# Moving the spread of a small low-rank factor from ScalarE to VectorE, and asking for it once in the middle of a product

## The reference, cut to what matters

```
x1  = x + W[cond[b]].T @ x                 # 128 x 2048
Bx  = x1 @ B[id[b]].T                      # 128 x 16   (sum over the 2048 times)
out = x1 + Bx @ A[id[b]].T                 # 128 x 2048
```

## Time and profile before

| | us |
|---|---|
| median of three runs | 393.79 |
| the profiled execution, its own time | 395.34 |
| its span, first to last instruction | 393.5 |
| between the two | 1.84 |
| PE busy in it | 376.5 |
| DVE / ACT / POOL busy in it | 230.8 / 238.4 / 112.2 |
| mean granted clock of PE | 0.982 of full |

### The profile page before, as it was taken

The page is one execution under the profiler, slowest core; times in us unless marked ns, Lnnn a source line. Parts: engine busy times, 40 slices in busy tenths (PEclk is TensorE's granted clock), DMA queues, the critical chain, the costliest instruction groups (busy, mean ns, idle before and its releaser), DMA issues.

```text
span 393.5 us, 16869 instructions
## 1 busy us (share of the span) xinstructions
PE 376.5 (96%) x6170; PEld 354.3 (90%) x6170; DVE 230.8 (59%) x447; ACT 238.4 (61%) x579; POOL 112.2 (29%) x260
## 2 busy tenths in 40 slices
PE   7989989999999999999999999999999999999981
PEld 7979979999999999999999999999999999999871
DVE  0226762676555667755566775556677555667763
ACT  1566644666656666665666666566666666666541
POOL 2122330333332223333222333322233332223210
PEclk9999988999999999999999999999999999999996
DMA  7999997999999999999999999999999999999567
GB/s 272 417 362 347 407 409 277 345 415 386 406 414 412 408 416 415 415 404 414 404 418 410 416 405 410 414 405 409 414 415 414 410 406 406 415 403 413 223 250 277
DMA packets 28383, 152.24 MB, mean 387 GB/s; under 512 B 3153, under 2 KB 3154, under 8 KB 12242
## 3 DMA queue, kind: packets, MB, share of 16 engines
q1 hardware_dynamic: 28226, 151.79, 96.1%
q10 hardware_dynamic: 144, 0.26, 0.2%
HBM read 84.94 MB, written 67.11 MB: 386 GB/s over the span
## 4 chain that ended last, share of the span: by engine, by line
PE 93%; DMA 2%; issue 2%; ACT 1%; DVE 1%; POOL 1%; SPq 0%; POOLq 0%; DVEq 0%; ACTq 0%
PE bank L388 60%; PE bank L428 16%; PE bank L404 16%; DMA x_in<-in_x 2%; POOL z_pair L218 0%; ACT x_out L300 0%; DVE x_out L319 0%; ACT z_all L268 0%; POOL z_all L223 0%; ACT ft L256 0%; DVE z_pair L335 0%; DVE z_part L312 0%; DVE z_all L339 0%; SPq L134 0%; SPq L133 0%
## 5 line engine op out<-in xcount | busy, mean ns | idle before, releaser
L388 PE MATMUL bank<-m_sel,x_in 128*128 128x128 f32 x2048 | 240.8, 279 | 2.9 <-ACT ft L256 1.7
L388 PEld LDWEIGHTS bank<-m_sel,x_in 128*128 128x128 f32 x2048 | 234.1, 194 | 8.6 <-DVE x_out L319 2.7
L256 ACT COPY ft<-bank 128x512 f32<-128x512 f32 x256 | 146.1, 587 | 65.5 <-PE bank L388 63.5
L319 DVE TENSOR_TENSOR x_out<-bank,ft 128x512 f32<-128x512 f32 x253 | 154.3, 681 | 19.6 <-PE bank L428 19.5
L218 POOL TENSOR_TENSOR z_pair<-z_part 16x128 f32<-16x128 f32 x126 | 54.2, 446 | 217.0 <-DVE z_part L312 198.6
L312 DVE COPY z_part<-bank 16x128 f32<-16x128 f32 x126 | 36.2, 287 | 121.2 <-PE bank L404 119.2
L268 ACT COPY z_all<-z_all 16x128 f32<-16x128 f32 x189 | 56.0, 296 | 46.9 <-POOL z_all L223 43.8
L428 PE MATMUL bank<-z_all,at 16*128 16x128 f32 x2048 | 70.0, 282 | 2.8 <-issue 1.8
L428 PEld LDWEIGHTS bank<-z_all,at 16*128 16x128 f32 x2048 | 63.2, 187 | 10.1 <-issue 10.0
L404 PE MATMUL bank<-ft,ab_in 128*16 128x128 f32 x2048 | 65.6, 274 | 1.6 <-issue 1.6
L404 PEld LDWEIGHTS bank<-ft,ab_in 128*16 128x16 f32 x2048 | 51.4, 96 | 10.6 <-issue 5.1
(11 more groups left out here) (7 smaller groups left out, 0.9 us busy)
## 6 DMA issues: line engine op xcount, KB each, us to landing
x_in<-in_x SPq DMA_DIRECT2D x63, 1024.0 KB, 11.3
out<-x_out SPq DMA_DIRECT2D x62, 1024.0 KB, 10.1
ab_in<-in_lora SPq DMA_DIRECT2D x64, 256.0 KB, 10.0
out<-x_out SPq DMA_DIRECT2D x3, 512.0 KB, 4.3
w_all<-in_weights SPq DMA_DIRECT2D x1, 1024.0 KB, 4.9
x_in<-in_x SPq DMA_DIRECT2D x2, 512.0 KB, 6.9
out<-x_out SPq DMA_DIRECT2D x1, 256.0 KB, 4.6
out<-x_out ACTq DMA_DIRECT2D x1, 256.0 KB, 5.9
```

The lines of the kernel that those rows point to most:

```text
L256: nc.scalar.copy(ft[k][u][:], bank[f_bank_of(kind, i, u, final)][:]).then_inc(copied, 1)
L319: nc.vector.tensor_tensor(x_out[k][:, UNIT * u:UNIT * (u + 1)], bank[banks[u]][:], ft[k][u][:], ALU.add).then_inc(added, 1)
L388: last = nc.tensor.matmul(to[:, P * c:P * (c + 1)], x_in[k][:, UNIT * u + P * c:UNIT * u + P * (c + 1)], m_sel[k][:], start=(c == 0), stop ...
```

## The change: what it does

1. `place_z` leaves ACT in all normal rounds and goes to DVE, in the round after, behind the two turns of A (L328) and ahead of `take_z`: six copies of 16x128 a round. For batch 62, and for the split work of batch 63, ACT keeps it.
2. PE's waits are put elsewhere. What stood ahead of L404 (A and B loaded, banks free, z taken) and of L428 (A turned, z summed, z placed, banks free) goes. In its place PE waits ahead of the last unit (u = 3) of the second batch's product, the round's eighth unit, for: z of b-2 and b-1 placed, the copies of batch b, and the x of the next round's first batch with its W. Between z of b and z of b+1 there is still the wait for ACT's last copies, and between the two low-rank products one for z taken.
3. In the end part PE asks for z of batch 61 ahead of the fourth unit of batch 62, and the z sums of batches 62 and 63 ask unit by unit for their copies.
4. The second batch's `take_z` counts on a semaphore of its own (z_odd_taken).

```
 ACT:
     for i in range(ROUND):
         take_z(i, b + i, Z_BANKS[i])
-    for i in range(ROUND):
-        place_z(ROUND * kind + i, b + i)
 DVE:
     for i in range(ROUND):
         turn_a(ROUND * kind + i, b + i, q + 1)
+    if begun(b - ROUND):
+        for i in range(ROUND):
+            place_z(ROUND * (1 - kind) + i, b - ROUND + i)
     for i in range(ROUND):
         take_z(i, b + i, Z_BANKS[i])
+def place_z(k, b):
+    dve.wait_ge(z_summed, b + 1)
+    for u in range(1, UNITS):
+        nc.vector.tensor_copy(z_all[k][rows_of_unit(u), :], z_all[k][rows_of_unit(0), :]).then_inc(z_placed, 1)
 PE, normal_round:
-    for i in range(ROUND):
-        mix_units(kind, i, b + i, q + 1, False)
-    for i in range(ROUND):
-        sum_z(k + i, b + i, q + 1, Z_BANKS[i], UNITS * (b - BODY + 1) + i + 1, b + i - 1)
-    if begun(b - ROUND):
-        add_low_rank(other, b - ROUND, LOW_BANKS[kind][0], UNITS * (b - ROUND), 0)
-        add_low_rank(other + 1, b - ROUND + 1, LOW_BANKS[kind][1], 0, b + ROUND)
+    for u in range(UNITS):
+        mix_unit(kind, 0, u, b)
+    ask_for_x(k + 1, b + 1, q + 1)
+    for u in range(UNITS):
+        if u == UNITS - 1:
+            if begun(b - ROUND):
+                ask_for_z(b - ROUND + 1)
+            else:
+                pe.wait_ge(a_turned, b + ROUND)
+            pe.wait_ge(copied, UNITS * (b + 1))
+            ask_for_x(other, b + ROUND, q + 1 + kind)
+        mix_unit(kind, 1, u, b + 1)
+    for u in range(UNITS):
+        sum_unit(k, u, b, Z_BANKS[0])
+    pe.wait_ge(copied, UNITS * (b + ROUND))
+    for u in range(UNITS):
+        sum_unit(k + 1, u, b + 1, Z_BANKS[1])
+    if begun(b - ROUND):
+        add_low_rank(other, LOW_BANKS[kind][0])
+        pe.wait_ge(z_odd_taken, 2 * (b + ROUND))
+        add_low_rank(other + 1, LOW_BANKS[kind][1])
+def ask_for_z(b):
+    pe.wait_ge(z_placed, (UNITS - 1) * (b + 1))
 PE, the end:
+    for u in range(UNITS):
+        if u == UNITS - 1:
+            ask_for_z(b - 1)
+        mix_unit(1, 0, u, b, True)
+    for u in range(UNITS):
+        pe.wait_ge(copied, UNITS * b + u + 1)
+        sum_unit(ROUND, u, b, Z_BANKS[0])
+    add_low_rank(0, LAST_LOW)
```

More of the change, by code:

```diff
@@ L106, in cond_lora_residual @@
         z_taken_dve = sem("z_taken_dve")
+        z_odd_taken = sem("z_odd_taken")
         z_paired = sem("z_paired")
@@ L212, in sum_z @@
                 parts = z_part[k % ROUND]
-                pool.wait_ge(z_taken_act, 2 * (b + 1))
-                pool.wait_ge(z_taken_dve, 2 * (b + 1))
+                if k % ROUND:
+                    pool.wait_ge(z_odd_taken, 2 * (b + 1))
+                else:
+                    pool.wait_ge(z_taken_act, b + 2)
+                    pool.wait_ge(z_taken_dve, b + 2)
                 if live(b):
@@ L262, in take_z @@
                 for c in (0, 2):
-                    nc.scalar.copy(z_part[i][c][:], rows_of_z(z_bank, c)).then_inc(z_taken_act, 1)
+                    nc.scalar.copy(z_part[i][c][:], rows_of_z(z_bank, c)).then_inc(z_odd_taken if i else z_taken_act, 1)
             def place_z(k, b):
@@ L311, in take_z @@
                 for c in (1, 3):
-                    nc.vector.tensor_copy(z_part[i][c][:], rows_of_z(z_bank, c)).then_inc(z_taken_dve, 1)
+                    nc.vector.tensor_copy(z_part[i][c][:], rows_of_z(z_bank, c)).then_inc(z_odd_taken if i else z_taken_dve, 1)
             def add_units(k, b, turns, banks, units=range(UNITS)):
@@ L333, in sum_last_z @@
                 for i in range(2):
-                    dve.wait_ge(z_taken_act, 2 * (BATCHES - 1) + i + 1)
+                    dve.wait_ge(z_odd_taken, 2 * (BATCHES - 2) + i + 1)
                     nc.vector.tensor_tensor(z_pair[i][:], rows_of_z(Z_BANKS[0], 2 * i + 1), z_part[1][2 * i][:], ALU.add
@@ L361, in _ @@
             turn_a(BODY - 1, BATCHES - 1, TURNS)
+            for i in range(ROUND):
+                place_z(i, BATCHES - BODY + i)
             take_z(0, BATCHES - 2, Z_BANKS[0])
@@ L370, in _ @@
         def _(pe):
-            def mix_units(kind, i, b, turns, final, units=range(UNITS)):
-                k = ROUND * kind + i
[L373 to L423, removed]
+            def ask_for_x(k, b, turns):
+                if isinstance(b, int) and b == 0:
+                    pe.wait_ge(first_loaded[0], 16)
+                else:
+                    pe.wait_ge(x_loaded[k], 16 * (turns - (k == 0)))
+                pe.wait_ge(m_picked, b + 1)
@@ new lines, in ask_for_z, with mix_unit @@
+            def ask_for_z(b):
+                pe.wait_ge(z_placed, (UNITS - 1) * (b + 1))
+            def mix_unit(kind, i, u, b, final=False):
+                k = ROUND * kind + i
+                if isinstance(b, int) and b == 0 and u > 0:
+                    pe.wait_ge(first_loaded[u // 2], 16)
+                if UNITS * i + u >= len(F_BANKS[kind]):
+                    behind = 1 if final and i > 0 and u == 0 else 3
+                    pe.wait_ge(copied, UNITS * b + u - behind + 1)
+                elif live(UNITS * (b - BODY) + u + 1):
+                    pe.wait_ge(added, UNITS * (b - BODY) + u + 1)
+                to = bank[f_bank_of(kind, i, u, final)]
+                for c in range(IN_UNIT):
+                    last = nc.tensor.matmul(to[:, P * c:P * (c + 1)],
+                                            x_in[k][:, UNIT * u + P * c:UNIT * u + P * (c + 1)], m_sel[k][:],
+                                            start=(c == 0), stop=(c == IN_UNIT - 1), skip_group_check=True)
+                last.then_inc(f_made, 1)
@@ L424, in add_low_rank, with sum_unit @@
+            def sum_unit(k, u, b, z_bank):
+                for c in range(IN_UNIT):
+                    first = RANK * (JS + IN_UNIT * u + c)
+                    last = nc.tensor.matmul(rows_of_z(z_bank, c), ab_in[k][:, first:first + RANK],
+                                            ft[k][u][:, P * c:P * (c + 1)], start=(u == 0), stop=(u == UNITS - 1))
+                if u == UNITS - 1:
+                    last.then_inc(z_done, 1)
+            def add_low_rank(k, banks, own=False):
                 for c in range(IN_UNIT):
@@ L451, in turn @@
                     normal_round(kind, q)
+            ask_for_x(0, 0, 1)
             turn(0)
@@ L457, in _ @@
             b = BATCHES - ROUND
[L458 to L466, removed]
+            for u in range(UNITS):
+                if u == UNITS - 1:
+                    ask_for_z(b - 1)
[4 more added lines that the diff above has]
+            add_low_rank(0, LAST_LOW)
+            ask_for_x(ROUND + 1, b + 1, TURNS)
+            for u in range(UNITS - 1):
+                mix_unit(1, 1, u, b + 1, True)
+            pe.wait_ge(added, UNITS * (b - 1))
+            add_low_rank(1, LAST_LOW)
+            mix_unit(1, 1, UNITS - 1, b + 1, True)
+            pe.wait_ge(z_taken_act, b + 2)
+            pe.wait_ge(z_taken_dve, b + 2)
+            for u in range(UNITS):
+                pe.wait_ge(copied, UNITS * (b + 1) + u + 1)
+                sum_unit(ROUND + 1, u, b + 1, Z_BANKS[0])
+            ask_for_z(b)
+            pe.wait_ge(added, UNITS * b)
+            add_low_rank(ROUND, LAST_LOW)
+            pe.wait_ge(z_summed, b + 1 + len(BY_DVE))
+            pe.wait_ge(z_placed, (UNITS - 1) * (b + 1) + len(BY_ACT))
+            pe.wait_ge(z_odd_taken, 2 * b + 2)
+            pe.wait_ge(z_paired, 2 * BATCHES)
+            add_low_rank(ROUND + 1, LAST_OWN, own=True)
 _INS = ['x', 'ids', 'weights', 'lora']
```

## The result

The changed kernel takes 415.5 us (median of four runs, 414.3 to 417.3) against 393.2 before (median of four as well): ratio 1.058, 95% interval 1.052 to 1.064. It is slower by 22 us. Its profiled execution has a span of 415.5 us and a time of 417.3.

A forecast was written before the change was run, and what follows sets the result against it. PE was taken to bound the kernel, the DMA queue close behind. Rounds +10.7, start -1.65, end part +3.0 and clock +1.0 made +13.0 us on 393.8: 407 us, range 395 to 419.

The forecast's parts named there:

- rival 1: The six placing copies on DVE cost 0.31 us each, the price of the L312 row: 417 us; chance 0.15.
- the forecast itself: PE waits for z ahead of the eighth unit in every round, 0.2 to 0.28 us a copy: 401 to 413 us; chance 0.60.
- Adds and turns, 6.10: DVE's part of the round's loop from the first add to the end of the turns of A: 6.10 us.
- A copy, 0.25: Each of DVE's six placing copies a round takes 0.25 us, between 0.16 and 0.31; six take 1.50.
- Hand-over and waits passed, 0.16: From DVE's last copy to PE's eighth unit: 0.06 us hand-over plus 0.10 for four more waits passed.
- Eighth unit to next first add, 4.06: PE's part of the loop: 4.26 us less 0.20 saved where stages lose their waits, making 4.06.
- +0.37: Lengthening of each round in the steady part: loop of 11.82 us against 11.45, over 29 rounds +10.7 us.
- The start, -1.65: In the second round PE's wait for ACT's late unit copies goes: gain 1.65 us, between 0 and 1.65.
- The end part, +3.0 and +1.0 for the clock: PE idles 4.1 us ahead of batch 62's fourth unit: net +3.0 us, plus 1.0 (0 to 3) for half-speed work.
- Rival 2: Copies are quick enough; the next x, asked for 5.0 us early at the eighth unit, binds: 398 to 401 us; chance 0.14.
- Rival 3: Not slower: the waits were the cost and the DMA queue speeds up with PE: 386 us; chance 0.08.
- Rival 4: The 0.6 us gap in each steady round lowers PE's clock; in a tenth of the rounds +30 us; chance 0.03.

## Why the prediction was right, point by point

Range and direction held (395 to 419; 415.5 measured), and the likeliest value, 407, was 8.5 us low. The number alone would have spoken for rival 1: 415.5 lies above the 401 to 413 that I gave the forecast itself and next to rival 1's 417, and the range held it only because it took in most of rival 1. The trace decides between them: the copies are 0.25 apart, not 0.31, and the missing time is elsewhere. The mechanism was the predicted one: a closed loop of DVE's adds, turns and copies and PE's eighth unit, z and low rank. The two experiments that open the loop in different places (copies ahead of the turns, asking later) both take away its cost (until the early ask for x binds), the one that adds copies lengthens it one for one, and the one that moves only the work costs nothing.

Its terms against the measurement:

- *Adds and turns, 6.10:* measured 6.12. *A copy, 0.25:* measured 0.223 long, six in 1.46, 0.25 apart. The middle of the two ends was the value; rival 1's 0.31 is out. The Trainium skill's two rules ("VectorE: DVE Perf Modes", "The perf-mode tier table" and "Two Vector instructions with no wait between them") agree with this: a length below that of the same shape from PSUM (0.288), and no overlap. The prediction put the missing overlap of the L312 pair down to the group of 32 partitions that is written. What the kernel shows to change there is the group that is read (`rows_of_z`); for the placing copies it is the group written, as said.
- *Hand-over and waits passed, 0.16:* measured 0.22. Asking for z last made it 0.09 less.
- *Eighth unit to next first add, 4.06:* measured 4.27. This is the step that failed. I had PE save 0.2 us there because two meetings lose their waits. Of the two, the one ahead of the z sums had no idle weight load before either (32 loads from 203.86, with no idle time noted in the row), so nothing could be saved there, and the one ahead of the low rank shows the same 0.21 us of idle weight load without any wait as with four (the earlier trace rows and the row at 213.51): it is not a cost of waiting. What did go is the gap in the middle of the z sums, where now all 64 weight loads stand in one piece of 1.66. And I had left out that a unit begun behind a blocked wait takes longer: from 210.56 to 211.64 it is 1.08 us, not 0.918. Gain and loss cancel, and 4.26 before became 4.27.
- So the round is +0.62 and not +0.37; over 29 rounds that is 7 us of those that the forecast lacked.
- *The start, -1.65:* measured -0.6. The wait for ACT's copies went, as said; but the first round now has a new gap of 1.07 us ahead of its eighth unit, where the x of batch 2 is asked for: it lands at 15.69 and the unit begins at 15.89, though the profile names ACT. In the runs that ask for x where it is used, this gap is absent. The prediction looked for the early ask only in the late rounds.
- *The end part, +3.0 and +1.0 for the clock:* measured +5.9 together. The gap was 3.94 for 4.1 predicted. The clock cost 3.9 us (10.06 against 6.18 at full clock for the same pieces of work), four times the predicted value and above the 3 that I had allowed at most. Without the clock the end part is 2.0 us longer and not 3.0: PE saves 1.9 us behind the gap, among it the 0.78 us that it had idled ahead of each of two z sums, where I had counted 1.1. The two errors partly cancel.
- *Rival 2* (copies quick enough, the early ask for x binds, load limited to 12.8 us, 398 to 401 us) didn't happen in the changed kernel but came true in each kernel in which z was in time: 398.1, 401.0 and 400.2 us, with loads of 12.9. That it was the x ask is shown by undoing it: 5.9 us less, or 5.0 against the kernel before measured beside each. The pace at which the DMA queue holds PE, forecast at 11.9 us a round, is 11.7 to 11.8.
- *Rival 3* (the DMA queue would follow PE) is refuted: with everything asked late PE's faster rounds of 11.27 run into the queue, and of the 7.5 us that it promised 2.5 are seen (390.0 against 392.5 for the kernel before, measured beside it). With fewer bytes the rounds stay fast. *Rival 4* (clock down in the steady part): the granted clock is 1.00 in every stretch between 80 and 370 us; the 0.54 us gaps do nothing to it. With longer gaps in the steady part it is not that safe: it fell behind two of 26 gaps of 2.04 us (twelve copies) and behind one of 0.93 us (all asked for where it is used).

What stays open: why nearly every kernel loses up to 6 us around 54 us, where PE stops for 1 to 2.6 us in the middle of a low-rank product with nothing that the profile names ahead of it, and then often works at half clock. It is in the old kernel (52.9 us) and in the new (53.9 us), at the end of the hardware loop's first pass. It was hardly there in the run with fewer bytes (0.8 us), but also small in the profiled execution in which only the end part asks late (1.0 us), with all bytes. It wasn't tried. Open too is what decides how long the clock stays down: with the same gap of 3.94 or 3.95 us in the end part it stayed at half for 10.3 us in the changed kernel and 10.2 with the copies ahead of the turns, but for 3.4 with z asked for later and with z asked for last. The end part took 31.0 us in the changed kernel and 28.7 in each of the last two.

## What to carry to other kernels

A step moved to an idle engine is free only as long as nobody asks for it early: add up the way round the loop, from the event that starts the moving engine's list to the unit that waits and back, and compare it with the round, not the busy shares. Gathering waits at one earlier point takes away slack from all that is asked for there, here 2.8 us from z and 5 us from x; in the rounds in which they bound they cost 0.80 and 0.50 us (12.07 and 11.77 against 11.27), more than all the waits they replaced, which had cost 0.18 us a round (11.45 against 11.27). And where a queue's time to landing grows through a run, the engine in front of it has less to gain than its own gaps say: it will meet the queue.

## What the runs showed of the hardware that I had not expected

- A float32 copy of 16x128 from SBUF to SBUF on VectorE took 0.223 us, the same from PSUM 0.287; neither overlaps with the next one.
- PE's change from the z sums to the low-rank product leaves the weight load idle for 0.21 us whether four waits stand there or none.
- A group of 8 passes begun behind a blocked wait took 1.08 us to the next stage's start, in an unbroken product 0.918; each satisfied wait behind the blocked one some 0.03 (an estimate, 0.09 over three).
- The length of a gap alone did not tell what PE's clock does. Within gaps of 3.94 or 3.95 us or right behind them it fell to 0.50 and stayed there for 10.3, 10.2, 3.4 and 3.4 us in four kernels. Of 26 gaps of 2.04 us in one kernel two were followed by a fall, of 3.4 us each. Two gaps of about 1 us within 2.1 us of each other were followed by none, one of 0.93 us by a fall of 3.4 us.
